# A gated cross-attention and mixture-of-experts layer: weight conversion moved to the end of each slot, projections one slot earlier, PSUM banks dealt out anew

## The reference, cut to what matters

```python
x = x + tanh(g_xattn) * xattn(layernorm(x), ctx, ctx, mask, Wq, bq, Wk, bk, Wv, bv, Wo, bo)
x = x + tanh(g_ffn)   * ffn(layernorm(x), W1, b1, W2, b2, Wa, Wb)
# xattn: q, k, v projections, scores / sqrt(16), masked softmax, attn @ v, @ Wo + bo
# ffn:   h = tanh(x.mean(axis=1) @ W1 + b1); probs = softmax(h @ W2 + b2); the 3 largest, renormalised
#        out = x + sum over these of w[e] * (gelu(x @ Wa[e]) @ Wb[e])      (256 -> 1024 -> 256)
```

## Time and profile before

| | before |
|---|---|
| median of 3 runs | 468.95 us (466.65 to 470.02) |
| the profiled execution, its own time | 467.19 us |
| its span in the trace | 465.4 us |
| TensorE matmuls busy | 365.0 us (78%) |
| ScalarE / VectorE / GpSimd busy | 195.3 / 177.0 / 161.1 us |
| start of the expert part (first L1146) | 311.68 us |

### The profile page before, as it was taken

How to read it: one execution, slowest core, us unless ns; L and a number is a source line. 1 busy time by engine, 2 the same in 40 slices (tenths; PEclk the granted TensorE clock), 3 DMA queues, 4 the chain that set the end, 5 groups by cost and what they waited for, 6 DMA issues and landing times.

```text
span 465.4 us, 8683 instructions
## 1 busy us (share of the span) xinstructions
PE 365.0 (78%) x3044; PEld 280.3 (60%) x3044; DVE 177.0 (38%) x560; ACT 195.3 (42%) x398; POOL 161.1 (35%) x219
## 2 busy tenths in 40 slices
PE   0623566775987958868789866969999999999996
PEld 0512234654755747656467654646887788888885
DVE  3112341353553735634636644332333322222222
ACT  0532133454444635444465534535345543343332
POOL 5865555645164265255443645610000000000000
PEclk9965666798888979978979989889999999999999
DMA  7353353344254354344443532310011011010000
GB/s 199 110 157 125 111 146 105 114 120 134 92 124 152 96 138 122 106 132 126 111 132 106 159 106 68 106 32 10 11 42 32 1 31 32 1 32 21 10 11 11
DMA packets 31769, 40.40 MB, mean 87 GB/s; under 512 B 8840, under 2 KB 25536, under 8 KB 31728
## 3 DMA queue, kind: packets, MB, share of 16 engines
q1 hardware_dynamic: 25024, 22.07, 16.7%
q0 software_dynamic: 4784, 16.98, 12.5%
q10 hardware_dynamic: 1920, 0.79, 0.7%
HBM read 33.09 MB, written 6.74 MB: 86 GB/s over the span
## 4 chain that ended last, share of the span: by engine, by line
PE 47%; DMA 32%; POOL 10%; DVE 5%; issue 3%; ACT 2%; SPq 1%; POOLq 0%; ACTq 0%; DVEq 0%
PE bank L1174 14%; PE bank L1146 13%; DMA kst<-k_scr 11%; DMA stage<-in_L_ffn_Wa 7%; DMA r_scr<-xr 7%; DMA k_scr<-k_hl 4%; PE bank L1156 4%; PE bank L986 3%; PE bank L952 2%; POOL wb L443 2%; POOL wa L443 2%; PE bank L972 2%; PE bank L962 2%; DMA xr<-in_x 2%; POOL stage L438 2%
## 5 line engine op out<-in xcount | busy, mean ns | idle before, releaser
L742 DVE CUSTOM_DVE_ANT_0 bank<-bank,maskb 112x375 f32<-112x375 f32 x128 | 67.9, 571 | 96.1 <-PE bank L952 95.6
L523 ACT ACTIVATE pT<-bank 125x448 f32<-125x448 f32 x96 | 51.5, 539 | 77.0 <-PE bank L986 59.1
L1146 PE MATMUL bank<-wa,ctxT 128*112 x288 | 71.4, 385 | 1.2 <-issue 1.2
L1174 PE MATMUL bank<-wb,stage 128*112 x576 | 67.0, 273 | 1.2 <-DVE stage L905 1.2
L952 PE MATMUL bank<-kst,qbd 128*112 128x375 f16 x128 | 40.8, 402 | 34.4 <-DMA kst<-k_scr 25.6
L905 DVE SCALAR_TENSOR_TENSOR stage<-bank,wbc,stage 128x448 f16<-128x448 f32 x48 | 32.7, 684 | 87.6 <-ACT stage L706 87.6
L1174 PEld LDWEIGHTS bank<-wb,stage 128*112 128x112 f16 x576 | 63.4, 130 | 4.2 <-issue 1.4
L972 PE MATMUL bank<-ms,pick 128*128 128x112 bf16 (+1 forms) x384 | 39.3, 231 | 25.7 <-ACT ms L592 25.7
L438 POOL TENSOR_SCALAR stage<-stage 128x512 f32<-128x512 f32 x64 | 39.4, 624 | 47.3 <-DMA stage<-in_L_ffn_Wa 28.6
L706 ACT ACTIVATE stage<-bank,wbc 128x448 f16<-128x448 f32 x48 | 30.1, 630 | 54.2 <-PE bank L1156 54.2
L972 PEld LDWEIGHTS bank<-ms,pick 128*128 128x128 bf16 (+1 forms) x384 | 32.6, 121 | 28.6 <-ACT ms L592 27.9
(11 more groups left out here) (116 smaller groups left out, 477.8 us busy)
## 6 DMA issues: line engine op xcount, KB each, us to landing
stage<-in_L_ffn_Wa POOLq DMA_DIRECT2D x16, 512.0 KB, 7.3
stage<-in_L_ffn_Wb POOLq DMA_DIRECT2D x16, 512.0 KB, 7.2
kst<-k_scr SPq DMA_DIRECT2D x32, 187.5 KB
ctx_s<-in_ctx SPq DMA_DIRECT2D x8, 375.0 KB
k_scr<-k_hl SPq DMA_DIRECT2D x16, 187.5 KB
qbd<-q_scr SPq DMA_DIRECT2D x32, 56.0 KB
xa<-in_x SPq DMA_DIRECT2D x8, 112.0 KB, 13.1
q_scr<-q_hl SPq DMA_DIRECT2D x32, 28.0 KB
```

The lines of the kernel that those rows point to most:

```text
L523: a.activation(pT[:, t % PRING, :], bank[0:CK, ST_BANKS[t % len(ST_BANKS)], 0:QUAD], ACT.Exp).then_inc(s["act_exp"], 1)
L742: v.tensor_tensor_reduce(out=bank[0:SQ, e, 0:SK], in0=bank[0:SQ, e, 0:SK], in1=maskb[:, b % 2, 0:SK], scale=-1.0, scalar=3.0e38, op0=ALU.a ...
L1146: ins = T.matmul(o, x2b[:, b % 2, xs * DT * SQ + t * SQ:xs * DT * SQ + (t + 1) * SQ], wa[:, bass.ds(e * (4 * CHUNK) + ws * (2 * CHUNK) + t ...
L1174: ins = T.matmul(o, hT[:, hs * FT * SQ + f * SQ:hs * FT * SQ + (f + 1) * SQ], wb[:, bass.ds(e * (4 * CHUNK) + ws * (2 * CHUNK) + f * D, D) ...
```

## The change

Six things are changed together.

1. Weights: `w_hi` moves behind all other ScalarE steps of a slot; GpSimd scales the parts of the next slot before it converts those of this one; `RING` grows from 4 to 6 parts. Iteration -2 converts nothing, iteration -1 converts 2 parts in each slot, and each later one 2, 2, 2, 1.
2. Projections: CX0, CX1 move from slot 1 to slot 0, K0, K1 from slot 2 to slot 1, with their ScalarE and VectorE steps.
3. PSUM: `st_tile` has banks 2, 3, 4 instead of 2, 3; the spare uses have 6, 7 instead of 4, 6, 7.
4. `PRING`, the ring of exponentiated tiles, grows from 4 to 5.
5. SP queue: `write_k` comes before `load_xr`, `load_mask` before `store_r`, `load_ctx` before `store_x2`.
6. Start: ScalarE normalises x of sequence 0 before it scales Wq, and scales bq only ahead of the first `q_hi`.

```diff
-RING = 4
-PRING = 4
+RING = 6
+PRING = 5
-ST_BANKS = (2, 3)
+ST_BANKS = (2, 3, 4)
-MISC_BANKS, TAIL_BANKS = (4, 6, 7), (6, 7)
+MISC_BANKS, TAIL_BANKS = (6, 7), (6, 7)
...
-    for i in range(-2, B):
+    for i in range(-1, B):
         for j in range(4):
-            n = (2 if j else 0) if i == -2 else 3 if i == -1 else 2 - j % 2
-            n = min(n, NPART - at)
+            n = min(2 if i < 0 or j < 3 else 1, NPART - at)
...
-        (("V0", n), ("XT", m), ("V1", n), ("X2T", b - 2), ("MX1", b)),
-        (("CX0", m), ("CX1", m), ("Q", m), ("OT", o)),
-        (("K0", m), ("ON", o), ("K1", m)),
+        (("V0", n), ("XT", m), ("V1", n), ("X2T", b - 2), ("MX1", b), ("CX0", m), ("CX1", m)),
+        (("Q", m), ("OT", o), ("K0", m), ("K1", m)),
+        (("ON", o),),
         (("MX0", n), ("OP", o)),
...
@@ sync
+                load_mask(m)
                 store_r(b - 2)
-                load_mask(m)
+                load_ctx(m + 1)
                 store_x2(b - 2)
-                load_ctx(m + 1)
                 write_q(m)
+                write_k(m, 0)
+                write_k(m, 1)
                 load_xr(o)
...
-                write_k(m, 0)
-                write_k(m, 1)
                 read_q(m, 0)
                 read_k(m, 0)
@@ gpsimd
                     ks = parts_at(b, slot)
-                    for k in ks:
+                    for k in parts_at(b + (slot + 1) // 4, (slot + 1) % 4):
                         scale_part(k)
@@ scalar
+            normed(0)
             act.wait_ge(s["wq_loaded"], 16)
-            act.wait_ge(s["bq_loaded"], 16)
...
-            normed(0)
@@ tensor
-                pe.wait_ge(s["wq_scaled"], 2)
+                pe.wait_ge(s["wq_scaled"], 1)
```

More of the change, by code:

```diff
@@ L239, in flamingo_layer @@
                  "k_written0 k_written1 q_written kq_in00 kq_in01 kq_in10 kq_in11 r_written x2_written "
-                 "part_loaded0 part_loaded1 scaled hi_done lo_done "
+                 "part_loaded0 part_loaded1 part_loaded2 scaled hi_done lo_done "
                  "pe_s1 pe_st pe_pv misc_full dve_max act_exp act_o parts_done ms_done xr_ready "
@@ L251, in flamingo_layer @@
         out_written = [s["out_written0"], s["out_written1"]]
-        part_loaded = [s["part_loaded%d" % i] for i in range(2)]
+        part_loaded = [s["part_loaded%d" % i] for i in range(RING // 2)]
         def tile(b, g, c):
@@ L468, in _ @@
                             base=0, pattern=[[-1, 128]], channel_multiplier=1).then_inc(s["ident_ready"], 1)
-            load_parts(0)
             norm1(0)
-            load_parts(2)
+            for k in range(0, RING, 2):
+                load_parts(k)
             pool.wait_ge(s["ident_ready"], 1)
@@ L631, in route_exp @@
                 a.activation(ez[0:n, :], lg[0:n, :], ACT.Exp, bias=nmx[0:n, :], accum_out=zs[0:n, :]).then_inc(s["e_done"], 1)
+            normed(0)
             act.wait_ge(s["wq_loaded"], 16)
-            act.wait_ge(s["bq_loaded"], 16)
             wq = wqkvo[:, 0, :, :].rearrange("p t n -> p (t n)")
             a.activation(wq, wq, ACT.Copy, scale=HD ** -0.5).then_inc(s["wq_scaled"], 1)
-            a.activation(bq_c[:, :], bq_c[:, :], ACT.Copy, scale=HD ** -0.5).then_inc(s["wq_scaled"], 1)
-            normed(0)
             for b in range(-2, B):
                 n, m, o = b + 1, b + 2, b - 1
-                ks = [list(parts_at(b, i)) + [NPART] * 3 for i in range(4)]
                 exp_tile(b, 0, 0)
@@ L644, in _ @@
                 o_copy(o)
+                exp_tile(b, 0, 2)
                 mask_bias(n)
-                exp_tile(b, 0, 2)
                 v_copy(n, 0)
                 xt_copy(m)
-                w_hi(ks[0][0])
                 v_copy(n, 1)
@@ L652, in _ @@
                 max_copy(b, 1)
-                w_hi(ks[0][1])
-                w_hi(ks[0][2])
+                cx_copy(m)
+                for k in parts_at(b, 0):
+                    w_hi(k)
                 exp_tile(b, 1, 0)
@@ L658, in _ @@
                 exp_tile(b, 1, 2)
-                w_hi(ks[1][0])
-                cx_copy(m)
-                w_hi(ks[1][1])
                 if b == -2:
+                    act.wait_ge(s["bq_loaded"], 16)
+                    a.activation(bq_c[:, :], bq_c[:, :], ACT.Copy, scale=HD ** -0.5).then_inc(s["wq_scaled"], 1)
                     act.wait_ge(s["wq_scaled"], 2)
@@ L665, in _ @@
                 q_hi(m)
-                w_hi(ks[1][2])
+                k_hi(m, 0)
+                k_hi(m, 1)
+                for k in parts_at(b, 1):
+                    w_hi(k)
                 if b == B - 1:
@@ L672, in _ @@
                 exp_tile(b, 2, 2)
-                w_hi(ks[2][0])
-                k_hi(m, 0)
                 ot_copy(o)
-                w_hi(ks[2][1])
-                k_hi(m, 1)
-                w_hi(ks[2][2])
+                for k in parts_at(b, 2):
+                    w_hi(k)
                 if b == B - 1:
@@ L684, in _ @@
                 exp_tile(b, 3, 2)
-                w_hi(ks[3][0])
                 max_copy(n, 0)
                 normed(m + 1)
-                w_hi(ks[3][1])
-                w_hi(ks[3][2])
+                for k in parts_at(b, 3):
+                    w_hi(k)
                 if b == -2:
@@ L870, in _ @@
                 o_rows(o)
+                if b == -2:
+                    dve.wait_ge(s["bk_loaded"], 16)
+                k_lo(m, 0)
+                k_lo(m, 1)
                 row_max(n, 2)
@@ L874, in _ @@
                 split_max(n, 0)
-                if b == -2:
-                    dve.wait_ge(s["bk_loaded"], 16)
-                k_lo(m, 0)
                 ln1_stats(m + 1)
-                k_lo(m, 1)
                 if b == B - 1:
@@ L1165, in g2 @@
                 if u == 0:
-                    pe.wait_ge(s[spare.last(4)[0]], spare.last(4)[1])
+                    pe.wait_ge(s["act_exp"], tile(B, 0, 0))
                 if u == TOPK:
```

## The result

The changed kernel takes 448.1 us (median of 4 runs, 447.7 to 449.0) against 467.8 us for the kernel before on the same chips: a ratio of 0.958 with a 95% interval of 0.953 to 0.963. It is 19.7 us faster, about half of the forecast 38.5, and inside the range. The profiled execution has a span of 445.9 us.

A forecast was written before the change was run, and what follows sets the result against it. Taken to bound: weight parts to about 84 us, then the keys' way through DRAM into `kst`, then TensorE. Span 235 + 38.2 + 153.7 = 426.9 us against 465.4; so 468.95 - 38.5 = 430 us, range 412 to 452.

The forecast's parts named there:

- The start, T(0) = 34: First row block of sequence 0, after its wait for `kst`, starts at 34 us, 7.7 earlier, with x normalised first.
- Fewer parts early, T(2) = 90: Converting 8 weight parts, not 18, before iteration 0: sequence 2's first row block starts at 90 us, 18.8 more gained.
- K a slot earlier: Key loop from K's projection through DRAM back to `kst`: net 3.1 us earlier, 31.2 to 28.1 a turn.
- load_xr: Read of `xr` on the SP queue, issued later, about 12 us into a turn, still lands before the residual; given nothing.
- A + 6.8 is the next T: Slot 0: from the end of `normed2` (A) to the next sequence's first row block (T) are 6.8 us.
- A waits for the load and GpSimd's scaling; turns of 29: `normed2` waits for GpSimd's second norm, behind scaling and its weight load; ends 22.9 us into a turn; turns of 29.
- Banks, 2 to 3 us an iteration: In slot 0, the third spare PSUM bank, now given away, was worth 2 to 3 us an iteration.
- The end, 38.2: From sequence 7's first row block to the expert part: 38.2 us, give or take 4, where it was 39.2.
- From there on it is the way of the keys: Kernel before, from about 84 us to the last key tile: K's low half, DRAM write, read into `kst` (13.6 us).
- Rival 1: Two busy DMA engines reading `kst` are the floor: turns of 31, no gain after sequence 2, 443 us; chance 0.18.
- Rivals 2 and 3: TensorE alone bounds, turns 26 to 27, 417 us, chance 0.20; conversions still hold ScalarE, 465 to 473 us, chance 0.05.
- Rival 4: GpSimd's second norm behind a weight load landing 15 us after issue: slower, 476 us at 16; chance 0.04.

The follow-up runs named there:

- read16: The changed kernel with each read of keys into `kst` split into two DMAs, 32 rows outermost instead of 2: 413.5 us, ratio 0.876.
- weights: The changed kernel with projections and `write_k` put back, and two score banks and three spare ones as before: 454.1 us, ratio 0.976.
- xr_two: The changed kernel with two buffers for `xr`, its load moved from behind `write_k` to the head of the iteration: 446.7 us, ratio 0.954.
- both: The changed kernel with the `kst` read split to 32 rows outermost and two `xr` buffers loaded at the iteration's head: 412.2 us, ratio 0.881.
- both_banks: The changed kernel with split `kst` reads, two `xr` buffers loaded at the iteration's head, and two score and three spare banks: 403.7 us, ratio 0.865.
- b_read16: The kernel before with only the `kst` read split into two DMAs with 32 rows outermost: 420.6 us, ratio 0.899.
- w_read16: The changed kernel with projections, `write_k` and banks put back as before, and the `kst` read split to 32 rows outermost: 393.0 us, ratio 0.842.

## Why the prediction was right in its range, and wrong in its likeliest case

- **The start, T(0) = 34: 38.2.** The norm came first and the low half ended at 17.5, where 18.2 was forecast. The step that failed here is "from there to T(0) it was 16.8, one weight load less, so 16": it took 20.7. `write_k` is issued at 18.25 and 19.12, the second write takes 7.25, the read 11.8. The read was shorter than the 12.9 us from its last issue to T(0) before; what grew are the four issues of `write_q` ahead of the write, and the write, which took 3.9 us before. The prediction took off 0.8 us for a weight load less beside this way; three were issued ahead of the write, where there had been two. What made the write slow stays open, but it isn't the reads of `kst`, since read16 has it too. What was saved on ScalarE was half lost here.
- **Fewer parts early, T(2) = 90: 98.0.** The mechanism held, and `weights` shows it without the projections and the banks: T(2) = 97.8. (It still has the norm first, the fifth `pT` tile and the swaps of `load_mask` and `load_ctx`.) Two turns took 59.8 where 56 was forecast; the rest of the miss is the start's.
- **K a slot earlier: 28.1 for the loop "all else equal".** This is the step that failed in the turns: the loop was to fall from 31.2 to 28.1 us, and the five turns average 31.0. K0 started at T + 5.2 (6.6 was forecast) and K1's low half ended at T + 9.2. All else was not equal, because the writes have to pass a queue that the reads of `kst` block. In xr_two, where `xr` no longer holds the turn, the issue of the write of T(3) waits behind `store_x2` and `write_q` until T + 10.8 (139.85 - 129.03), and write and read take another 18.9, which makes 29.7. Over the five turns of xr_two against those of the kernel before, K1's low half ends 3.0 us earlier (T + 10.3 against 13.3 on average), its write is issued 1.4 us earlier (T + 11.9 against 13.4), and the last read of half 0, which waits for that write, is issued at T + 18.2 in both. The 3 us were gone before the read began. The five turns are 2.6 us shorter together, where 15.5 were forecast for this term alone.
- **`load_xr`: "I give it nothing; late by 2 us it would cost those 2".** It was issued as forecast and landed at T + 19 where about T + 17 was needed. That was so in two turns, and made A = T + 25.7 and 26.6 in place of 22.9, and the turns 32.4 and 33.2. But the price of that was nil or near it, as xr_two shows: without it the turns are 29.7 to 32.4 for all but the last, and the keys end most of them.
- **A + 6.8 is the next T.** 6.7 in the changed kernel (155.33 to 162.01). The waits of V1, MX1 and CX0 stand where the prediction put them, 0.58, 0.37 and 0.67 us at T(3).
- **A waits for the load and GpSimd's scaling; turns of 29.** The number is right in read16, where the mean of the five is 28.8, and in one turn of the changed kernel (29.6). The reason given for it is not: GpSimd's scaling in slot 3 did not wait for its load, but stood behind `add_bo` and the low halves of slot 2, which follow the row maxima. That this, too, gives A = T + 22.0 on average in read16 is luck.
- **Banks, 2 to 3 us an iteration.** By the medians of `both` and both_banks it is 8.5 us over all. In their traces, of which that of `both` was of its slowest run, it is 11.1: 5.1 ahead of T(2) and 6.3 in the five turns, 1.3 a turn. Those come ahead of A, by way of K0, and not in slot 0, where the prediction has them.
- **The end, 38.2: 39.4,** within its 4 us.
- **"From there on it is the way of the keys", for the kernel before.** That holds up to T(5) only. From there the chain that ended last goes by the residual's buffer: `xr` can't be loaded again before the store to `r_scr` has landed, and that takes 14.4 and 15.9 us behind the reads of `kst`:

```profile
239.90 14.35 DMA r_scr<-xr
254.26 2.01 DMA xr<-in_x
...
266.67 15.94 DMA r_scr<-xr
282.62 1.83 DMA xr<-in_x
```

With the split alone (b_read16) the same store lands in 2.0 to 4.1 us in these turns. So the reads of `kst` held two ways to the end of a turn, and the prediction priced one.

**Rival 1 is what happened, in its outcome**: "a turn is 31 and nothing is gained after T(2)". It had 0.18. Its parts are only roughly so: it has the writes landing at T + 16 and a read of 15 us, and in xr_two, at T(3), they are T + 18.0 and 11.6. The sign that the prediction named for it, `kst` still ending the wait with turns over 30, is not in the changed kernel at T(3) to T(6); it took xr_two and read16 to see it. Its 443 lacks the 8 us by which T(2) is later; the five turns were 2 us shorter than its 157, the end 1.2 longer. The row that spoke for it was the share of 0.12; what spoke against it, a turn of 28.3, is the last turn, which is short (25.9 to 29.2) in every kernel here with the slow read. The Trainium skill ("DMA: Bandwidth & Descriptors", section "Rules for kernel authors") says that such a leading dimension keeps a transfer to at most as many engines as it is long. That agrees with the 0.12 and with what the split gives. The prediction had the mechanism, its row and its price, and gave it too little weight, because beside the read's own length it asked only when K's writes can land, and not what else has to pass through the queue while it runs. The writes, `store_x2` and `load_xr` all do. Rivals 2 and 3 did not occur. Rival 4 did not either, by its own sign, a weight load of 15 us; but its place was right, since the second norm did stand behind a late load, that of `xr`.

That the result lies in the range is owed to the range, which took in rival 1 with its 443, and only in part to the likeliest mechanism: ahead of T(2) that gave 18.5 us where 26.5 were forecast, and in the turns 1 us where 11 were.

What is argued and not shown: how the reads slow the other transfers. That their form does it is shown, since read16 and b_read16 change nothing else; that it is by pieces which wait on the two busy engines is not. And the 10.7 us between both_banks and w_read16 are those of the projections, of `write_k` and of the buffers for `xr` together, of which the last were worth 1.3 between read16 and `both`.

One thing in the description of the change has to be read with care: `w_hi` stands behind all other ScalarE steps of a slot but `normed2`, which in slot 3 still follows it.

## What to carry to other kernels

A transfer that uses few of the engines costs more than its own length: look at how long each later issue on its queue takes, and what lands late behind it, before moving anything to an earlier place in that queue. Moving the producer of a slow chain earlier gains only what the slow chain isn't sharing; repair the transfer first, then measure again what each part of the change is worth, since here the projections' new place was worth some 5 us with the slow read, and with the fast one it belongs, with the banks, to what costs 16 to 20 us. Which of the two ways to write the projections is better can't be read from the kernel before. And a resource (the third spare bank) that is free to give away under one bound costs 9 us under the next.

## What the runs showed of the hardware that was not expected

- An issue on the SP queue can itself take long. That of a 112 KB store took 0.3 to 0.9 us in the kernel before, up to 6.2 in the changed one and up to 9.1 in xr_two, where it stood right behind the reads of `kst` on two engines, and 0.3 to 0.5 with them split (read16). The kernel before had long ones too, of other transfers: 4.8 us for a load of x, 4.4 for a read of `kst`.
- A 112 KB store that was issued behind the two-engine reads landed after 12.7 to 15.9 us (`r_scr` in the kernel before, in the five turns from T(2) on). The same store landed after 2.0 to 4.1 with the reads split (b_read16), and after 1.85 in the kernel before at 296.31 us, with no read of `kst` before it.
- The same 750 KB of reads a sequence, with 960 packets more out of some 32,000 over the kernel, landed in 2.1 to 6.2 us (read16 and b_read16, in pieces of 94 KB; a half within 3.7 to 10.2 of its first issue) where a half took 10.7 to 13.6 from its last issue in the chains. With what hung on them, this took 47 us out of the kernel before.
